# Where the maximum passes stand in a step of the second cross attention

## What is computed

```python
q = (x @ Wq).reshape(b, n, H, DH)
k = (context @ Wk * SCALE).reshape(b, m, H, DH)
v = (context @ Wv).reshape(b, m, H, DH)
scores = jnp.einsum('bihd,bjhd->bhij', q, k)
attn = jax.nn.softmax(scores, axis=-1)
out = jnp.einsum('bhij,bjhd->bihd', attn, v)
return out.reshape(b, n, H * DH) @ Wo + bo
```

## Time and profile before

| | |
|---|---|
| time, median of 3 runs | 6000.6 us (5981.24 to 6007.14) |
| profiled execution, time | 6004.0 us |
| its span, first to last instruction | 6002.2 us |
| mean granted TensorE clock | 0.890 of full speed |
| PE busy | 5247.9 us (87%) |
| DVE busy | 4108.1 us (68%) |
| ACT busy | 2587.5 us (43%) |
| maximum reductions of the stage, L1137 | 1664, 1086.8 us |
| probability sums, L1167 | 768, 936.2 us |

### The profile page before, as it was taken

The page is one execution under the profiler, slowest core; times in us unless marked ns, Lnnn a source line. Parts: engine busy times, 40 slices in busy tenths (PEclk is TensorE's granted clock), DMA queues, the critical chain, the costliest instruction groups (busy, mean ns, idle before and its releaser), DMA issues. The chain is left out here.

```text
span 6002.2 us, 67570 instructions
## 1 busy us (share of the span) xinstructions
PE 5247.9 (87%) x19735; PEld 2604.6 (43%) x19735; DVE 4108.1 (68%) x6066; ACT 2587.5 (43%) x4954; POOL 782.0 (13%) x702
## 2 busy tenths in 40 slices
PE   7888787978888797887978999999999999999994
PEld 2333453535445353543334444444444444444442
DVE  3666665647466564744647888888888888888875
ACT  1444553536455363641442444444444444444441
POOL 0000442424234242420010000000000000000000
PEclk7778888888888888885778999999999999999996
DMA  0000000000000000000000000000000000000000
GB/s 17 3 0 0 29 11 9 1 19 1 17 3 11 9 2 18 1 1 10 1 24 4 2 1 4 1 3 3 3 3 3 3 1 4 1 3 3 1 1 8
DMA packets 18045, 35.02 MB, mean 6 GB/s; under 512 B 3418, under 2 KB 12250, under 8 KB 16746
## 3 DMA queue, kind: packets, MB, share of 16 engines
q1 hardware_dynamic: 17642, 30.22, 1.6%
HBM read 29.69 MB, written 0.52 MB: 5 GB/s over the span
## 5 line engine op out<-in xcount | busy, mean ns | idle before, releaser
L1137 DVE TENSOR_REDUCE xat_part<-xat_ring 128x1 f32<-128x512 f32 (+1 forms) x1664 | 1086.8, 668 | 260.3 <-PE xat_ring L969 241.4
L1080 ACT ACTIVATE xat_p_full<-xat_sc 128x1024 f32<-128x1024 f32 (+1 forms) x816 | 835.2, 1024 | 963.3 <-PE xat_sc L1015 959.8
L1167 DVE TENSOR_TENSOR xat_p_sum<-xat_p_sum,xat_p_full 128x1024 f32<-128x1024 f32 x768 | 936.2, 1219 | 43.1 <-ACT xat_p_full L1080 35.6
L996 PE MATMUL xat_acc<-xat_p_full,xat_v 128*64 128x512 f32 (+1 forms) x3264 | 883.2, 619 | 1.3 <-ACT xat_p_full L1080 1.2
L969 PE MATMUL xat_ring<-xat_k_hl,xat_q_hh 128*128 128x512 f32 (+1 forms) x1664 | 717.0, 446 | 53.7 <-DVE xat_k_hl L1134 18.4
L1014 PE MATMUL xat_sc<-xat_q_hh,xat_k_hl 128*128 128x512 f32 (+1 forms) x1632 | 750.1, 460 | 0.0
L1015 PE MATMUL xat_sc<-xat_q_lm,xat_k_h 128*128 128x512 f32 (+1 forms) x1632 | 648.8, 398 | 0.0
L969 PEld LDWEIGHTS xat_ring<-xat_k_hl,xat_q_hh 128*128 128x128 f32 x1664 | 312.6, 189 | 709.4 <-issue 335.1
L1686 DVE TENSOR_REDUCE loc_peak<-loc_sc 128x2 f32<-128x320 f32 x384 | 188.3, 490 | 495.8 <-PE loc_sc L1434 492.2
L1536 ACT ACTIVATE loc_probs<-loc_sc,loc_peak 128x160 f32<-128x160 f32 x768 | 294.0, 387 | 501.0 <-DVE loc_peak L1686 493.4
L1593 POOL TENSOR_TENSOR loc_probs<-loc_probs,loc_rinv 128x320 f32<-128x320 f32 x384 | 353.3, 920 | 863.6 <-DVE loc_rinv L1691 860.2
(11 more groups left out here) (386 smaller groups left out, 7702.6 us busy)
## 6 DMA issues: line engine op xcount, KB each, us to landing
loc_w_qkv<-in_L_ffn_w SPq DMA_DIRECT2D x6, 1536.0 KB, 6.5
loc_w_o<-in_L_ffn_wo SPq DMA_DIRECT2D x6, 512.0 KB, 3.2
xat_ctxT<-in_ctxT SPq DMA_DIRECT2D x12, 256.0 KB, 2.7
xat_w_qk<-in_L_xattn_wqk SPq DMA_DIRECT2D x16, 128.0 KB, 2.0
loc_w<-in_L_ffn_w SPq DMA_DIRECT2D x6, 341.0 KB, 3.0
loc_w<-in_L_ffn_w SPq DMA_DIRECT2D x6, 192.0 KB, 2.4
loc_rope<-in_rope SPq DMA_DIRECT2D x1, 1024.0 KB
xat_w_o<-in_L_xattn_wo SPq DMA_DIRECT2D x16, 64.0 KB, 1.8
```

Of the source, the lines that this page charges most:

```text
L996: last = pe.matmul(acc[h * GROUP:(h + 1) * GROUP, e, :], v[0:size, t, e * GROUP:(e + 1) * GROUP], p_full[0:size, t % 3, cols(h)], start=(t ...
L1080: act.activation(p_full[0:size, j % 3, :].rearrange("p (a b) -> p a b", a=2), sc[0:size, x:x + 2, :], ACT.Exp, scale=GROUP ** -0.5).then_i ...
L1137: ins = dve.tensor_reduce(part[:, t, c:c + 1], ring[:, b, 0:chunks[c][1]], AX.X, ALU.max)
L1167: dve.tensor_tensor(p_sum[:, e, :], first_in, p_full[:, (j - 1) % 3, :], ALU.add)\
```

## The change

Every maximum pass of a step is put into `mid`. Before, passes of even number stood there and those of odd number in `post`. K, V, U, Y and T keep their steps and places.

```diff
                 for n in range(NCH * NTOK):
-                    steps[4 + n * 45 // (NCH * NTOK)][post if n % 2 else mid] += [("M", order[n // NTOK], n % NTOK)]
+                    steps[4 + n * 45 // (NCH * NTOK)][mid] += [("M", order[n // NTOK], n % NTOK)]
                 steps[NT - 2][post] += [("T", 0, 0), ("T", 1, 0)]
```

## The result

| | before | after |
|---|---|---|
| time, median of 4 runs | 6003.87 us (5981.24 to 6007.99) | 6146.8 us (6135.34 to 6160.1) |
| profiled execution, time | 6004.0 | 6146.85 |
| its span | 6002.2 | 6145.1 |
| first score of head 0 to that of head 15 | 2504.8 | 2650.3 |

The change makes the kernel slower by 2.5%: the ratio is 1.0247, with an interval of 1.0213 to 1.028. The forecast was 6119 us with a range of 6070 to 6170, so the time lies within it, 28 us above the forecast. (The table ahead of the prediction had three runs of before; a fourth, 6007.99, has come to them.) The whole difference lies in heads 0 to 14: 145.5 us of the profiled 142.8 (head 0 began 3.9 us earlier in this execution).

A forecast was written before the change was run, and what follows sets the result against it. PE was taken as the bound, DVE close behind. Even heads +8.0 us, odd +7.4, head 0 +9.6; seven, seven and one make 56 + 52 + 10 = 118 us on a 6000.6 median: 6119 us, range 6070 to 6170.

The forecast's parts named there:

- Plain two-pass steps: Steps with two passes and nothing else, 23 a head: cost nothing, stay 2.60 us, with 0.09 us of DVE slack.
- Three-pass steps: 14 a head: third pass waits 0.72 us for the first one's buffer; with later weighting 0.82 us a step.
- K steps: Steps with a key projection: second pass waits for K's buffer, costing 0.53 us with two passes, 1.00 with three.
- Steps 10 to 48: Sum of array time and waits over these steps: +7.1 us in an even head, +6.0 in an odd one.
- The order of steps 4 and 5: Around the reciprocal, one 3.04 us gap becomes gaps of 1.5 and 2.1; 12.60 us becomes 12.5, nothing won.
- The clock: Slow clock behind the gaps of steps 4 and 5: 0.9 us added a head, bounds 0 and 1.5.
- Steps 7 to 9: Around the outputs: step 7 0.8 us shorter, step 8 0.8 longer; odd heads pay 0.5 in step 9.
- Rival 2: Kernel gets faster, 5940 us: covering the reciprocal in steps 4 and 5 outweighs the ring waits elsewhere; chance 0.06.
- Rival 3: Three-pass steps already lose as much to DVE's lateness as to the ring; only K steps add, 6021 us; chance 0.08.
- Rival 4: Slow clock in the 14 three-pass steps a head adds 82 us, giving 6201 us; chance 0.06.

The follow-up runs named there:

- the first experiment: The changed kernel, but from step 10 on the third pass of a step stands behind the weighting again; 6046.85 us, 1.0058 of before.

## Why the prediction was right, and where it was off

- **Plain two-pass steps, 0.** Held: 2.60 before and after. DVE had the slack: in step 19 of head 2 it stood idle for 0.18 us ahead of its first reduction, where I had counted 0.09.
- **Three-pass steps, 0.82.** Held for step 23 (3.65, made of 2.84 of array time and 0.81). The chain of 0.43 and 0.75 from the earlier trace rows was exact.
- **K steps, 0.53 and 1.00.** Read in pairs, since K lies ahead of its step's first score. Steps 16 and 17 of even heads: array 2.84 + 2.60 + 0.86, waits 0.82 + 0.53, forecast 7.65, measured 4.22 + 3.41 = 7.63. Steps 12 and 13: 2.60 + 2.84 + 0.86 + 1.00 = 7.30, measured 3.16 + 4.14 = 7.30.
- **Steps 10 to 48, +7.1 and +6.0.** Measured +6.98 and +5.87. Building the new step from array time and all its waits was safer than adding to today's step, because today's steps 20, 29, 32 and 45 have waits of their own, which the change removes or replaces.
- **The order of steps 4 and 5, 12.60 to 12.5.** Held in even heads without the clock: 12.61 with the gaps filled. But "nothing is won" set a time without low clock against one with it. With the gap filled in either order, steps 4 to 6 take 14.2 in the order before and 15.2 now in even heads, 14.6 and 15.6 in odd ones: the order itself costs 1.0 us a head.
- **The clock, +0.9 a head with bounds 0 and 1.5.** This is the term that was most mis-sized, and it lies outside its bounds. Filled gaps saved 2.2. I took less than one slow stretch of the old length; but after the change two gaps of 1.5 and 2.1 us follow each other with one pass between, the low clock meets the weighting, V and the scores, and it lasts into step 6.
- **Steps 7 to 9, 0 (odd heads +0.5).** Measured +0.43 and +1.18. Step 7 gained 0.7 of the 0.8 it was given (5.33 to 4.60 in even heads), but step 8 lost 1.3, not 0.8 (3.79 to 5.06). Outputs and step 8 of head 2, after:

```profile
3623.31 1.13 PE L988 MATMUL xat_ring<-xat_o,xat_w_o 64*128 64x512 f32 x4
...
3626.26 0.39 PE L969 MATMUL xat_ring<-xat_k_hl,xat_q_hh 128*128 128x260 f32 x1 [0.57 <-DVEq L1149]
...
3628.06 1.12 PE L953 MATMUL xat_ring<-xat_ctxT,xat_w_qk 128*128 128x512 f32 x2 [0.41 <-DVE xat_part L1137]
```

  The second pass starts 2.95 behind the outputs, as the 1.96 and 0.99 of the earlier trace rows said. K then waits too, and only the sum of both was mis-sized.
- **Step 49**, not in the sum, adds 0.1 a head.

The sum of the misses: 1.3 for the clock, 0.1 (even) and 0.2 (odd) for the order of steps 4 to 6, 0.4 and 0.7 for steps 7 to 9 and 0.1 for step 49, less the tenth by which steps 10 to 48 came out lower, is 1.8 in even and 2.2 in odd heads, 28 us in all; 118 + 28 = 146.

**The rivals.** Rival 2 (faster) fell: the cover of the reciprocal brought nothing, as DVE's owed work did reach step 5's second pass, and the third pass cost 0.81, not the 0.56 from which it would decide. Rival 3 (only K adds) fell with the first experiment: putting third passes behind gave 100 us back. But its observation was half right, since today's three-pass steps do lose time to DVE and to the ring; the experiments took 4 us a head of it. Rival 4 (low clock in three-pass steps) fell: the clock was 1.00 in steps 10 to 48 of all heads, at a gap of about 0.55 in each three-pass step. The Trainium skill's warning ("TensorE: Matmul & The Clock Gate", section "A second HAM failure mode: psum-queue depth-cycling") is not borne out by those short gaps. What lowers the clock here are the two long gaps of step 5, once a head, and there filling them brought it back.

What stays open is when exactly the clock falls and rises: steps 4 and 5 of odd heads took 12.43, 12.70, 12.76 and 13.71 us in four kernels with the same order there.

## What to carry to other kernels

With a ring of two buffers, count for every item the start-to-start time from the item two places ahead of it to that one's last read; here a pass needs 1.18 us and K 2.55. Work that has to be done anyway and stands between the two (here the 1.01 us of weighting) covers that time. Put elsewhere, it leaves PE to wait for the rest in each step, even if every item could start earlier. Split by the place within a step, not by the parity of a running number: from step 10 on, two ahead and one behind, K's partner behind, plain steps all ahead, gives 1.2% on one chip and 0.8% on another, with the same instructions. And when a gap of some microseconds can't be removed, look at the clock behind it; discarded matmuls in the gap may pay.

## What the hardware showed that I had not expected

- Two gaps of 1.5 and 2.1 us, with one matmul between, brought the granted clock from 0.98 to 0.50 for 4 us and 0.67 for the next 4, while gaps of about 0.55 us in the twelve three-pass steps from step 10 on left it at 1.00. Matmuls whose results are overwritten, six and eight in the gaps, kept it at 1.00, and made the kernel 30 us faster.
- A lead of 0.2 us that DVE wins in plain steps, where no wait shows it, shortened the next three-pass step ahead of a K by 0.2 to 0.3 us in even heads and 0.4 in odd ones, where the K step behind it took 0.17 back.
